# A four-layer image network with routed experts on one core: expert tiles of the first six images beside the routing of the last, biases added outside TensorE, a guard on pairs of tiles

## The reference, cut to what matters

```python
def _L0_ffn_ref(h, gate_w, gate_b, w1, b1, w2, b2):          # 8 experts, one a token, hidden 512
    probs = softmax(x @ gate_w + gate_b); idx = argmax(probs); prb = probs[idx]
    pos = position of the token among those of its expert; kept = pos < C
    hmid = relu(einsum('ecd,edf->ecf', buf, w1) + b1[:, None, :])
    ybuf = einsum('ecf,efd->ecd', hmid, w2) + b2[:, None, :]
    y = nan_to_num(ybuf[idx, pos] * (prb * kept), nan=0.0, posinf=10000.0, neginf=-10000.0)
def _L1_ffn_ref(...):   # 8 experts, the two best a token, hidden 512, exact gelu, biases b1 and b2
def _L2_ffn_ref(...):   # 8 experts, the two best a token, hidden 256, exact gelu, biases b1 and b2
def _L3_ffn_ref(...):   # 16 experts, the two best: silu(x @ w1) * (x @ w2), then w3; no bias
```

## Time and profile before

| | us |
|---|---|
| median of 3 runs | 2589.05 (2588.59 to 2589.72) |
| profiled execution, its whole time | 2590.67 |
| its span in the trace | 2588.9 |
| PE busy | 1772.6 |
| DVE busy | 1695.7 |
| ACT busy | 1056.6 |
| POOL busy | 1061.8 |
| granted clock of TensorE, mean over the span | 0.836 |

### The profile page before, as it was taken

How to read it: one execution, slowest core, us unless ns; L and a number is a source line. 1 busy time by engine, 2 the same in 40 slices (tenths; PEclk the granted TensorE clock), 3 DMA queues, 4 the chain that set the end, 5 groups by cost and what they waited for, 6 DMA issues and landing times. The chain is left out here.

```text
span 2588.9 us, 44772 instructions
## 1 busy us (share of the span) xinstructions
PE 1772.6 (68%) x10287; PEld 1291.4 (50%) x10304; DVE 1695.7 (66%) x4992; ACT 1056.6 (41%) x2271; POOL 1061.8 (41%) x993
## 2 busy tenths in 40 slices
PE   1476333399348888389998157629974999929992
PEld 1232233388334433178887124318863544419992
DVE  6998699488757777434443677636648577765664
ACT  2333465277233333145554213304434444416661
POOL 0143133244102334434444307747763055546662
PEclk9788655599669999699999668759996999959996
DMA  2000100121210001121111411113324101113236
GB/s 67 0 1 1 65 24 25 42 64 55 74 66 16 24 28 34 42 64 58 57 59 38 140 35 50 49 54 103 95 90 163 37 32 34 34 54 94 85 89 205
DMA packets 171900, 151.82 MB, mean 59 GB/s; under 512 B 28958, under 2 KB 151590, under 8 KB 171746
## 3 DMA queue, kind: packets, MB, share of 16 engines
q1 hardware_dynamic: 141794, 90.82, 12.1%
q0 software_dynamic: 29952, 59.26, 6.5%
HBM read 83.77 MB, written 68.79 MB: 59 GB/s over the span
## 5 line engine op out<-in xcount | busy, mean ns | idle before, releaser
L1033 POOL DMA_INDIRECT returned<-channel_major x488 | 481.0, 986 | 456.3 <-DVE channel_major L992 325.0
L878 PE MATMUL psum<-channel_major 128*128 128x128 f32 x3360 | 461.3, 278 | 0.9 <-ACT channel_major L925 0.9
L941 ACT ACTIVATE channel_major<-psum,bias_columns 128x128 f32<-128x128 f32 x1104 | 323.2, 367 | 293.6 <-PE psum L878 292.9
L894 PE MATMUL psum<-expert_weights,channel_major 128*128 x2784 | 427.9, 289 | 0.6 <-DVE channel_major L981 0.6
L878 PEld LDWEIGHTS psum<-channel_major 128*128 128x128 f32 x3360 | 421.2, 195 | 1.1 <-issue 1.1
L706 POOL DMA_INDIRECT dispatched<-rows_first_choice,slot x192 | 191.8, 999 | 530.0 <-DVE rows_second_choice L632 366.6
L894 PEld LDWEIGHTS psum<-expert_weights,channel_major 128*128 128x128 f32 x2784 | 349.3, 191 | 25.1 <-issue 1.9
L706 POOL DMA_INDIRECT dispatched<-rows_second_choice,slot x192 | 195.4, 1018 | 67.5 <-issue 65.4
L992 DVE TENSOR_SCALAR channel_major<-psum,channel_major 128x128 f32<-128x128 f32 x416 | 144.9, 348 | 97.7 <-PE psum L894 93.1
L969 DVE COPY channel_major<-expert_weights 128x512 f32 (+1 forms) x272 | 100.0, 368 | 157.6 <-PE psum L878 150.6
L326 PE MATMUL psum<-identity,rows_first_choice 128*128 128x128 f32 x256 | 41.5, 322 | 195.4 <-DVE rows_first_choice L313 182.6
(11 more groups left out here) (338 smaller groups left out, 3456.6 us busy)
## 6 DMA issues: line engine op xcount, KB each, us to landing
channel_major<-dispatched SPq DMA_DIRECT2D x488, 65.0 KB
expert_weights<-returned SPq DMA_DIRECT2D x12, 1024.0 KB, 10.4
rows_second_choice<-returned SPq DMA_DIRECT2D x8, 1024.0 KB, 10.8
returned<-channel_major POOLq DMA_INDIRECT x488
expert_weights<-in_L_ffn_w SPq DMA_DIRECT2D x3, 2048.0 KB, 8.9
residual<-in_x SPq DMA_DIRECT2D x8, 512.0 KB, 7.2
rows_first_choice<-returned SPq DMA_DIRECT2D x4, 1024.0 KB, 8.8
out<-residual SPq DMA_DIRECT2D x8, 512.0 KB, 6.0
```

The lines of the kernel that those rows point to most:

```text
L878: ins = pe.matmul(k.ps[:, PSH + u % 2, j * P:(j + 1) * P], wc[:, u % 2, j * P:(j + 1) * P], xt[:, u % 2, :], start=True, stop=True)
L894: ins = pe.matmul(bank, gs[:, u % HB, j * P:(j + 1) * P], second[:, bass.ds(e, 1), j, :].rearrange("p a c -> p (a c)"), start=(b2 is None ...
L941: ins = act.activation(hs[:, u % HB, cols], k.ps[:, PSH + u % 2, cols], f["act"], bias=bcol[:, bass.ds(e * J + j, 1)])
L1033: pool.indirect_dma_start(out=k.returned[0:N * K, :], out_offset=bass.IndirectOffsetOnAxis(ap=rt[:, u, C:C + 1].bitcast(I32), axis=0), in_ ...
```

## The change

1. The block `experts` is gone. A class `Experts` gives each engine its part, called at the end of the mixer's own part, so there is one block a layer after `norm_mixer`.
2. There are two tables of tiles. The first holds only whole tiles of the rows of images 0 to 5 (40 tiles in layer 0, 80 in the others) and is worked out after `place` of image 5 (`plan_first`). The second holds the rest (32, 56, 56 and 64 tiles), from all eight images (`plan_second`). The loop over experts is replaced by a comparison on all partitions with a sum along the row (`columns`); SP brings each table to one row by two DMAs (`load_table`).
3. SP loads 16 tiles as soon as six images have been sent, then broadcasts the second biases, then loads up to tile 31 (layer 0) or 63. Then come the second table, the pads, a wait for both, and the rest of the tiles.
4. PE, DVE and ACT do the pieces of the last image's routing within the first tiles, by the table `TAILS`; POOL sends its rows two (layer 0: one) before each result of tiles 8 to 15, 9 to 16 or 12 to 19.
5. Biases: ACT multiplies the bias row of the expert by the token's weight (one more activation a tile), and DVE adds it while it scales (L1088). The matmul L891 is gone. The first biases are loaded with one DMA of single elements, early in the mixer.
6. Results use two PSUM banks, since routing uses banks 6 and 7, and PE waits until the one of two tiles before was read. The rings stand in the rows of the first six images.
7. The guard of layer 0 works on two tiles at a time.

```diff
+FIRST_IMAGES = 6
+FIRST_TILES = [8 * FIRST_IMAGES - 8, 16 * FIRST_IMAGES - 16, 16 * FIRST_IMAGES - 16, 16 * FIRST_IMAGES - 16]
+TAILS = [
+    dict(pe=(0, 4, 5, 7), dve=(0, 2, 6, 8, 9), act=(2, 4, 7), send=8),
+    dict(pe=(0, 4, 5, 8), dve=(0, 2, 6, 9, 10), act=(2, 4, 7), send=9),
+    dict(pe=(0, 6, 8, 12), dve=(0, 3, 9, 13, 14), act=(3, 6, 10), send=12),
+    dict(pe=(0, 6, 8, 12), dve=(0, 3, 9, 13, 14), act=(3, 6, 10), send=12),
+]
...
+    def sync(self, sp):
...
+        route.load_table(sp, 0)
+        sp.wait_ge(*route.when("rows_sent", 16 * TPB * self.K * FIRST_IMAGES))
+        for u in range(RING):
+            load(u, u)
+        if self.b2 is not None:
+            sp.dma_start(self.b2rows.rearrange("p e c -> p (e c)"),
+                         self.b2.rearrange("e c -> (e c)").partition_broadcast(P)).then_inc(self.s["bias_rows"].h, 16)
+        with sp.Fori(1, self.split) as g:
+            for u in range(RING):
+                load(g * RING + u, u)
+        route.load_table(sp, 1)
+        self.route.send_pads(sp)
+        sp.wait_ge(*route.when("rows_sent", 16 * TPB * self.K * B))
+        sp.wait_ge(*route.when("pads_sent", 16 * self.E))
+        with sp.Fori(self.split, self.T // RING) as g:
...
+        def result(t, u):
+            e = self.expert_of(pe, t)
+            pe.wait_ge(*self.when("gated_ready" if self.gated else "act_ready", t + 1))
+            if past(t, 2):
+                pe.wait_ge(*self.when("y_read", t - 1))
-                if b2 is not None:
-                    pe.matmul(bank, k.ones[0:3, :], bp2[:, bass.ds(e, 1), :].rearrange("p a f -> p (a f)"),
-                              start=True, stop=False)
...
+            act.activation(self.wb[:, u % 4, :], self.b2rows[:, bass.ds(e, 1), :].rearrange("p a c -> p (a c)"), ACT.Copy,
+                           scale=self.rt[:, u, C + 1:C + 2]).then_inc(self.s["bias_weighted"].h, 1)
...
+        self.weights_here(act)
+        act.wait_ge(*route.when("table_loaded", 32))
+        act.wait_ge(self.s_row[0].h, self.s_row[0].base + 16)
+        if self.b2 is not None:
+            act.wait_ge(*self.when("bias_columns", 16))
+            act.wait_ge(*self.when("bias_rows", 16))
...
+                ins = dve.scalar_tensor_tensor(out=self.ys[:, u, :], in0=self.result_bank(u), scalar=weight,
+                                               in1=self.wb[:, u % 4, :], op0=ALU.mult, op1=ALU.add)
...
+        def step(t, u, last):
...
+            if at == add:
+                route.add(dve, B - 1)
+            if at == norm:
+                (route.invert if route.scalar_norm else route.norm)(dve, B - 1)
+            if at == choose:
+                route.choose(dve, B - 1)
+            if at == place:
+                route.place(dve, B - 1)
+            if at == plan:
+                route.plan_second(dve)
...
+        for t in range(T):
+            u = t % RING
+            if t == start:
+                route.slots_known(pool, B - 1)
+            if 0 <= t - start < TPB:
+                route.send_tile(pool, B - 1, t - start)
+            pool.wait_ge(*self.when("y_guarded" if self.guard else "y_read", t + 1))
+            pool.indirect_dma_start(
```

More of the change, by code:

```diff
@@ L401, in __init__ @@
         self.T = N * K // P + E
+        self.first_tiles = FIRST_TILES[layer]
         self.G = E + K - 1
@@ L668, in root @@
+        self.columns(ch, dve, 1, n)
+        self.plan_ops += ch.n
     def root(self, act, b):
@@ L696, in exp, with send_tile, slots_known @@
         act.activation(self.exo[:], self.ex[:], ACT.Exp).then_inc(self.s["exp_ready"].h, 1)
-    def send(self, pool, b):
+    def send_tile(self, pool, b, t):
+        for c in range(self.K):
+            pool.indirect_dma_start(
+                out=self.k.dispatched,
+                out_offset=bass.IndirectOffsetOnAxis(ap=self.slot[:, b % 2, c, t:t + 1], axis=0),
+                in_=self.rows[c][:, b * TPB + t, :], in_offset=None).then_inc(self.s["rows_sent"].h, 16)
+    def slots_known(self, pool, b):
         K = self.K
@@ new lines, in tensor, with turn_rows, hidden @@
+    def tensor(self, pe):
+        k, f, route, s_row = self.k, self.f, self.route, self.s_row
+        def turn_rows(t, u):
+            pe.wait_ge(s_row[u].h, s_row[u].base + (t - u) * (16 // RING) + 16)
+            pe.transpose(k.ps[:, self.PSX + u % 2, 0:P], self.rt[:, u, 0:C], k.ident[:]).then_inc(self.s["x_turned"].h, 1)
+        def hidden(t, u):
+            pe.wait_ge(*self.when("x_copied", t + 1))
+            if not self.vector_copies:
+                pe.wait_ge(*self.when("w_copied", t + 1))
+            for j in range(self.wide // P):
+                ins = pe.matmul(k.ps[:, self.PSH + u % 2, j * P:(j + 1) * P], self.wc[:, u % 2, j * P:(j + 1) * P],
+                                self.xt[:, u % 2, :], start=True, stop=True)
+            ins.then_inc(self.s["hidden_ready"].h, 1)
+        def result(t, u):
[3 more added lines that the diff above has]
+                pe.wait_ge(*self.when("y_read", t - 1))
+            for j in range(self.J):
+                ins = pe.matmul(self.result_bank(u), self.gs[:, u % self.HB, j * P:(j + 1) * P],
+                                self.second[:, bass.ds(e, 1), j, :].rearrange("p a c -> p (a c)"),
+                                start=(j == 0), stop=(j == self.J - 1))
+            ins.then_inc(self.s["y_ready"].h, 1)
+        back, rows, gate, rank = self.tail["pe"]
+        def step(t, u, last):
+            at = t if isinstance(t, int) else -1
+            if not last:
+                turn_rows(t + 1, (u + 1) % RING)
+            if at == rows:
+                route.turn_rows(pe, B - 1)
+            if at == gate:
+                route.gate(pe, B - 1)
+            if at == rank:
+                route.rank(pe, B - 1)
+            if past(t, 2):
+                result(t - 2, (u - 2) % RING)
+            hidden(t, u)
+        route.turn_back(pe, B - 1)
+        self.weights_here(pe)
+        turn_rows(0, 0)
+        self.tiles(pe, step)
+        result(self.T - 2, (self.T - 2) % RING)
+        result(self.T - 1, (self.T - 1) % RING)
@@ new lines, in done @@
+    def done(self):
+        k, T = self.k, self.T
+        k.advance(x_turned=T, x_copied=T, w_copied=0 if self.vector_copies else T, hidden_ready=T, act_ready=T,
+                  y_ready=T, y_read=T, weights_loaded=self.loads)
+        if self.gated:
+            k.advance(gated_ready=T)
+        if self.guard:
+            k.advance(guard_step=3 * T, y_guarded=T)
+        if self.b2 is not None:
+            k.advance(bias_columns=16, bias_rows=16, bias_weighted=T)
+        for r in range(RING):
+            self.s_row[r].base += 16 * self.uses[r]
+            self.s_out[r].base += 16 * self.uses[r]
```

589 lines of the change are left out of this document (306 added, 283 removed).

## The result

The kernel after took 2452.43 us (median of four runs, 2447.67 to 2455.78), the kernel before 2589.2 beside it: ratio 0.947, 95% interval 0.9458 to 0.9481, which is 136.8 us less. A second set of runs gave 2453.48 against 2588.09, ratio 0.9478 (0.9463 to 0.9494). The forecast was 2438. The profiled execution has a span of 2448.8, which is 140.1 less than before. Its busy line, to be held against the earlier trace rows: PE and DVE each lost about 60 us of work, ACT gained 99 with the new bias activation.

The account below looks back on a forecast made before the run. Tile loops were taken as bound by PE in layers 0, 1 and 3, nearly by POOL in 2. Layer gains 38 + 84 + 14 + 15 = 151 us off the 2588.9 span gave 2438 against the median, range 2395 to 2505.

Parts of the forecast that it names:

- The bias matmul, 0.34 a tile: PE's tile loops: dropping L891 saves 0.34 us a tile, 46 us in layer 1 and 14 us in layer 0.
- layer 0's bound: Layer 0's tiles: ACT needs at least 2.05 us against PE's 1.91, so only 14 us are saved.
- First tiles: Layers 0 and 1 start tiles before the last image is routed: at 467, not 503.1, and 1054.5, not 1105.6.
- the routing within the first tiles: Layer 1: the last image's routing, put into the tiles, costs 12 us, bounds 3.7 and 25.
- Layer 0's switch of tables: Layer 0 before row 32: 17.5 to 18 us covered by 14 tiles' 28.7 less POOL's lag of 4 to 10.
- Layer 2: POOL is the chain at 1.289 us a result; layer 2 gains 14 us and PE's saving is not seen.
- Layer 3: Last result at 2531 instead of 2546.5, with 80 tiles at 1.446 us after the switch: gain 15 us.
- The stall ahead of row 64: Layer 3: PE waits some 16 us for row 64, behind the second table and pads in SP's queue.
- at nothing: Two banks for four, rings in image rows and bias loads cost nothing; failing by 0.1 a tile in layers 0 and 1: 21 us.
- the forecast 2410: Layer 3: time when row 64 is ahead of PE, summed as 2381.6 + 1.6 + 0.5 + 26.3.
- Rival C: Layer 2: each POOL result waits for DVE's whole weight copy, pace 1.58, 44 us longer, 2482; chance 0.07.
- Rival D: Layers 1 and 2: ACT reloads its table twice a tile at 1.28 each, 585 us more, about 3023; chance 0.03.

Follow-up runs that it names:

- experiment 2: The kernel before with bias matmul L891 left out and nothing in its place, run on two chips: ratio 0.9735 on one, 0.9691 on the other.
- f4: The kernel before without the bias matmul, second biases left out, run again beside a control: 2507.98 us, ratio 0.9691.
- experiment 4: The kernel after, with the second table and pads issued between loads of the last first-table tiles: 2427.58 us, ratio 0.9377.
- experiment 5: The kernel after, with DVE scaling result t-2 before copying rows t+1, and PE's bank wait gone except in the last tile: 2464.58 us, ratio 0.951.
- e5: The kernel before without the bias matmul, on the chip where the kernel before took 2788 us: 2717.78 us, ratio 0.9735.
- The control: The kernel after, unchanged, run again beside later kernels on a chip like the first: 2453.48 us.

## Why the prediction came close, and where it was off

The direction and the main mechanisms held: 137 us less where 151 were forecast. That the sum came this near is in part luck. Against the forecast the layers are off by -1.7, +9.7, -5.7 and -14.7 us, so layer 1 made up for half of what layers 2 and 3 fell short, and layer 0 is near only because a pace that was too slow in the forecast (10 us) cancels a late first tile, dearer routing and an unpriced wait at the switch of tables. Point by point:

- **The bias matmul, 0.34 a tile: right.** 0.35 put back or taken out. The forecast saved it in 136 tiles in full and only 0.2 a tile in layer 0. The term that was mis-sized is layer 0's bound: I summed ACT's durations to 2.05. ACT's rows after, one tile of layer 0:

```profile
472.35 1.15 ACT L1024 ACTIVATE rows_first_choice<-psum,bias_columns 128x128 f32<-128x128 f32 x4 [1.68 <-PE psum L962]
473.37 0.42 ACT L1027 ACTIVATE rows_first_choice<-rows_first_choice,rows_second_choice 128x128 f32 x1
473.66 0.64 ACT L1007 ACTIVATE rows_first_choice<-expert_weights 128x512 f32 x1
474.27 0.89 ACT L1024 ACTIVATE rows_first_choice<-psum,bias_columns 128x128 f32<-128x128 f32 x3
```

  The durations sum to 2.21, but each starts before the one ahead has ended: from start to start it is 474.27 - 472.35 = 1.92, the pace of PE. That gave (2.05 - 1.915) x 72 = 10 us more than forecast. The expectation that DVE with a guard for every tile needs 2.0 to 2.05 was wrong in another way: its 129.80/68 = 1.9 before was busy time, in which overlap is not counted twice, and the same work took 72.05/40 = 1.8 of busy time a tile in experiment 2 (f4), which fits into 1.90.
- **First tiles: right in kind.** ACT's first work in layer 0 came at 469.4, forecast 467, because the broadcast took 5 us to land and not 3. In layer 1 it came at 1017.2, where 1054.5 less the 36.3 that layer 0 had gained is 1018.2. The term that was mis-sized there is the routing within the first tiles, priced at 12 us: counted from ACT's first work, the first 16 tiles took about 5 us over the pace. With the earlier start (1 us) and a pace of 1.892 in place of 1.91 (2.4 us) that is nearly all of the 9.7 us that layer 1 gave beyond the forecast.
- **Layer 0's switch of tables: wrong.** It was called covered, "though in layer 0 barely". PE waited 4.28 us in one piece, and tiles 24 to 40 cost 7 us over the pace; in experiment 4, with the pads between the loads, they took 1.91 and 1.96 a tile. The covering time was worked out with 2.05 a tile, which the tiles did not need, and POOL's lag there includes the guard of a pair.
- **Layer 2: too high by 6.** From the end of image 6's sends to the twelfth result POOL took 35.3 us, forecast 29, because it stood 6.9 and 6.5 us idle behind the broadcast and 7.7 more beside the routing. The rest took 188 us where 184 were forecast, with 5.3 us at the switch of tables where 3 were counted. Image 6's sends ended 4 us earlier than forecast, which gave a part of this back.
- **Layer 3: the step that failed.** The stall ahead of row 64 was right in kind (16 forecast, 13.5 measured). But the 80 tiles after it were priced at 1.446 and took 1.54. What was costed "at nothing" held PE's wait for the bank, which I had looked at only as a wait (the bank is read in time, and it is), not as one more instruction in PE's queue. That is 7.6 us there, of which 1.0 is that the kernel before took 1.458 and not 1.446; taking the wait away gave 8.5 us back in these tiles (experiment 5). Row 64 came 3 us later than forecast and its group of eight took 4 us over the pace. The sum behind the forecast 2410 has a slip: its terms from the second table to row 64 add up to 24.7, not 26.3, so by them row 64 was due at 2408.4 and came 4.6 later.
- **Rival C: out.** POOL in layer 2 sends at 0.98 + 0.30 in the kernel after too, beside DVE's weight copies (groups by line from 1620 to 1680 us: count, busy time and mean ns of one, idle time before):

```profile
L1157 POOL DMA_INDIRECT returned<-rows_second_choice x40 | 39.4, 986 | 12.2 <-issue 8.5 <-DVE rows_second_choice L1088 3.7
```

```profile
L1063 DVE COPY rows_first_choice<-expert_weights 128x256 f32 x38 | 13.6, 359 | 18.1 <-PE psum L962 11.6 <-issue 6.3
```

  DVE pays: its copy takes 359 ns on the mean and 300 in the kernel before, POOL's DMA 986. The Trainium skill (SBUF — State Buffer, "SBUF: two separate sides") says that the one that starts first holds the shared ports. The traces agree in that both are seen to take longer, but POOL only by 0.12 us now and then: 8 of 136 results in layer 2 before are over 1.05 us, and none after.
- **Rival D: out.** The new activation (L1027) has no table load at all, and the one that it alternates with (L1024) has six in the whole run:

```profile
L1024 ACT ACT_TABLE_LOAD x6 | 7.7, 1283 | 39.4 <-DMA rows_first_choice<-in_L_ffn_b 33.7 <-issue 5.6
```

## What to carry to other kernels

When tiles are let start earlier, walk the in-order queue that feeds them (here SP's) and ask of every DMA in it who needs it first: moving one broadcast ahead of 16 loads and spreading 16 pads gave 33 and 25 us, together over a third of what the whole change gave. On the engine that bounds, look for the small instructions first: one matmul of three rows was worth 65 to 80 us here. Price a wait that is always met as an instruction of its engine's queue: on PE in layer 3, which runs without a gap and has 13 matrix instructions a tile, it cost 1.541 - 1.457 = 0.08 us a tile, and in layer 1, with 17, nothing. And where an engine is near the bound, take its cycle from start to start, not as a sum of durations.

## What was not expected of the hardware

- A bfloat16 matmul of three rows by 128 columns costs 0.35 us in a row of float32 ones that take 0.112 each. The trace of the kernel before shows where: it starts 0.20 us behind the turn, the first matrix instruction of the result 0.16 behind it, and the second 0.21 behind the first; without it the first matrix instruction of the result starts 0.11 behind the turn and the second 0.11 behind the first. 0.20 + 0.16 + 0.21 - 0.22 = 0.35. Whether the three rows or the change of type does it was not tested.
- One of the chips ran the kernel before in 2788 us and not 2589 (11 runs, 2782 to 2802), with the granted clock about the same (0.83). Without the bias matmul (e5 against f4), layer 2's tiles took 1.4 to 1.9 us there where POOL's 1.29 was the pace on the other chip; the instructions took as long (POOL's results 0.986 us against 0.992 on the mean), the time is between them. Why is open. The control was not run on that chip, so what the change is worth there isn't known.
